# Layer 3's local attention: cosine products straight from PSUM in two halves, inverse norms by one power on GpSimd, and new instruction orders for slots 34 to 56

## The reference, cut to what matters

```python
qkv = h @ wqkv                      # 128 -> 3 x 512, eight heads of 64
q = l2norm(q) * qs; k = l2norm(k) * ksc
q = q * cos * scale + rotate_half(q) * sin * scale
k = k * cos / scale + rotate_half(k) * sin / scale
o = local_attention(q, k, v)        # windows of 64, each sees itself and the one before
def l2norm(t): return t / clip(norm(t), 1e-12)
```

## Time and profile before

| what | value |
|---|---|
| median of 3 runs | 3129.53 us (3119.51 to 3137.19) |
| span of the profiled execution | 3123.3 us |
| PE busy | 2749.7 us, 88% |
| DVE busy | 2224.2 us, 71% |
| ACT busy | 1703.5 us, 55% |
| POOL busy | 794.2 us, 25% |

### The profile page before, as it was taken

How to read it: one execution, slowest core, us unless ns; L and a number is a source line. 1 busy time by engine, 2 the same in 40 slices (tenths; PEclk the granted TensorE clock), 3 DMA queues, 4 the chain that set the end, 5 groups by cost and what they waited for, 6 DMA issues and landing times.

```text
span 3123.3 us, 66472 instructions
## 1 busy us (share of the span) xinstructions
PE 2749.7 (88%) x25741; PEld 1757.8 (56%) x25741; DVE 2224.2 (71%) x5316; ACT 1703.5 (55%) x4158; POOL 794.2 (25%) x809
## 2 busy tenths in 40 slices
PE   6878898899998899998878998999998889899998
PEld 3556665544455544467745887565653332455665
DVE  4766567788877677765566446889787777788884
ACT  2344533656622466543466434767765566767773
POOL 1010001111112111111232114646431112555550
PEclk8889997999999999998999989999999888999999
DMA  3523310000000000037500565010100000101001
GB/s 108 226 46 69 71 42 1 1 1 1 1 1 1 1 1 1 14 133 275 206 6 4 189 236 172 15 28 15 26 17 3 1 1 1 25 16 26 17 18 26
DMA packets 134803, 159.51 MB, mean 51 GB/s; under 512 B 82901, under 2 KB 109781, under 8 KB 132954
## 3 DMA queue, kind: packets, MB, share of 16 engines
q1 hardware_dynamic: 131962, 150.08, 15.7%
q0 software_dynamic: 2048, 4.20, 0.4%
q10 hardware_dynamic: 480, 0.98, 0.1%
HBM read 106.53 MB, written 30.61 MB: 44 GB/s over the span
## 4 chain that ended last, share of the span: by engine, by line
PE 47%; DVE 24%; ACT 10%; issue 8%; POOL 4%; DMA 3%; SPq 0%; DVEq 0%; POOLq 0%; ACTq 0%; another core or an unknown queue 0%
DVE nm L1221 5%; PE ps L1180 3%; PE ps L1955 3%; PE ps L1121 3%; PE ps L1157 3%; PE ps L565 3%; ACT hand L529 3%; PE ps L2157 3%; PE ps L418 2%; PE ps L2323 2%; PE ps L642 2%; DVE pre L2243 2%; PE ps L297 2%; PE ps L263 2%; PE ps L1551 1%
## 5 line engine op out<-in xcount | busy, mean ns | idle before, releaser
L1221 DVE TENSOR_REDUCE nm<-ps 128x2 f32<-128x256 f32 (+2 forms) x704 | 424.5, 637 | 87.1 <-PE ps L1121 50.1
L1270 ACT ACTIVATE core<-ps 128x512 f32<-128x512 f32 x672 | 359.1, 590 | 93.9 <-PE ps L1162 59.1
L359 POOL TENSOR_TENSOR rstd<-ve,weights 128x4 f32<-128x4 f32 x80 | 83.2, 1040 | 941.7 <-DVE ve L336 878.5
L2229 POOL TENSOR_TENSOR pre<-pre,sin 128x512 f32<-128x512 f32 x128 | 234.8, 1854 | 226.3 <-ACT pre L2200 199.6
L1121 PE MATMUL ps<-hand 128*128 128x128 bf16 (+4 forms) x1024 | 246.2, 315 | 44.0 <-DVE nm L1221 39.2
L529 ACT COPY hand<-ps 64x512 bf16<-64x512 bf16 x336 | 195.2, 581 | 126.7 <-PE ps L565 77.6
L1157 PE MATMUL ps<-hand 128*128 128x128 bf16 (+4 forms) x1024 | 223.0, 305 | 14.6 <-ACT hand L529 9.2
L2363 ACT ACTIVATE core<-ps,nm 128x128 f32<-128x128 f32 x512 | 182.5, 381 | 62.8 <-DVE nm L2380 62.0
L2234 POOL TENSOR_TENSOR ss<-ss,weights 128x16 f32<-128x16 f32 x64 | 195.9, 3061 | 71.0 <-DVE ss L2249 69.2
L2157 PE MATMUL ps<-weights,pre 128*128 128x512 f32 x384 | 203.2, 632 | 7.6 <-ACT pre L2203 4.5
L263 PE MATMUL ps<-identb 128*128 128x256 bf16 x1180 | 182.3, 283 | 18.3 <-PEq L3008 14.0
(11 more groups left out here) (348 smaller groups left out, 6693.3 us busy)
## 6 DMA issues: line engine op xcount, KB each, us to landing
hand<-in_experts SPq DMA_DIRECT2D x72, 836.0 KB, 6.7
shear<-post SPq DMA_DIRECT2D x64, 256.0 KB
core<-in_experts SPq DMA_DIRECT2D x16, 836.0 KB, 8.0
core<-shear SPq DMA_DIRECT2D x128, 64.0 KB, 2.2
hand<-hand SPq DMA_DIRECT2D x16, 512.0 KB, 4.4
hand<-hand SPq DMA_DIRECT2D x16, 384.0 KB, 5.6
pre<-sorted_in SPq DMA_DIRECT2D x8, 704.0 KB, 5.1
sorted_out<-core SPq DMA_DIRECT2D x88, 64.0 KB
```

Of the source, the lines that this page charges most:

```text
L1221: nc.vector.tensor_reduce(nm_of(unit), src, AX.X, ALU.max, negate=True).then_inc(negmax, 1)
L1270: nc.scalar.activation(prob8[:, i % PROBS, 0:w], m.ps[:, RING[at % NR], 0:w], ACT.Exp).then_inc(ring_out, 1)
L2229: ins = nc.gpsimd.tensor_tensor(o[:, :, :, z:z + hl], x[:, :, :, y0:y0 + hl], sn[:, t, :, z:z + hl].unsqueeze(2).to_broadcast([P, 2, LH, h ...
```

## The change

In `l3_layer_pre`:

- DVE's cosine product reads q and k from their PSUM banks instead of from `raw3`, in two instructions of 512 elements. Each waits until ACT has copied and squared the bank. PE may fill a bank that held q or k again only after this product (`rotated`).
- The inverse norm comes from POOL alone: a clamp of the sums of squares at 1e-24, then the power -0.5. The clamp and the reciprocal on DVE go.
- POOL's sine product of tile t waits for the addition of tile t-1 instead of its reciprocal; ACT's copy of tile t no longer waits for the cosine product of tile t-2.
- The constant 0.5 goes, and the constant -0.5 becomes wider.

The orders of slots 34 to 56 are new, those of the other slots the same (their text is only broken at other places). Core and finish are unchanged, and so is the preparation of the full attention.

```diff
+        def rotated(at):
+            for t in range(NT):
+                for i in range(2):
+                    if fill_of(t, i) == at:
+                        pe.wait_ge(cosed, 2 * t + i + 1)
...
             pe.wait_ge(lane.taken, max(at - N + 1, f))
+            rotated(at - N)
             nc.tensor.matmul(banks[at % N], s.hT[:, t * P:(t + 1) * P], qkv[:, l, i, :], start=True, stop=True).then_inc(lane.filled, 1)
...
             pe.wait_ge(lane.taken, at - N + 1)
+            rotated(at - N)
...
                         if i == 0 and t >= 2:
-                            act.wait_ge(cosed, t - 1)
                             act.wait_ge(sined, t - 1)
...
                     if t >= 1:
-                        pool.wait_ge(step, 3 * t)
+                        pool.wait_ge(step, t)
...
             pool.wait_ge(summed, t + 1)
-            nc.gpsimd.tensor_tensor(m.ss[:, 1, 0:2 * LH], m.ss[:, 0, 0:2 * LH], m.weight["half"][:, 0:2 * LH],
+            if t >= 1:
+                pool.wait_ge(roped, t)
+            nc.gpsimd.tensor_scalar(m.ss[:, 0, 64:64 + 2 * LH], m.ss[:, 0, 0:2 * LH], 1e-24, None, ALU.max).then_inc(held, 1)
+            pool.wait_ge(held, t + 1)
+            nc.gpsimd.tensor_tensor(m.ss[:, 1, 0:2 * LH], m.ss[:, 0, 64:64 + 2 * LH], m.weight["neg_half"][:, 0:2 * LH],
                                     ALU.pow).then_inc(rooted, 1)
...
-            yield T * t + 4.5
-            dve.wait_ge(copied, 2 * t + 2)
-            if t >= 2:
-                dve.wait_ge(lane.filled, fill_of(t - 2, 4) + 1)
-            nc.vector.tensor_tensor(heads(s.qt[:, t % 2, :]), heads(s.raw3[:, t % 2, :]),
-                                    cs[:, t, :, :].unsqueeze(2).to_broadcast(full), ALU.mult).then_inc(cosed, 1)
+            for i in range(2):
+                yield T * t + 3.0 + 1.7 * i
+                if t >= 2 and i == 0:
+                    dve.wait_ge(lane.filled, fill_of(t - 2, 4) + 1)
+                dve.wait_ge(lane.taken, fill_of(t, i) + 1)
+                nc.vector.tensor_tensor(heads(s.qt[:, t % 2, :])[:, i],
+                                        banks[fill_of(t, i) % N].rearrange("p (h e) -> p h e", e=LHD),
+                                        cs[:, t, i, :].unsqueeze(1).to_broadcast([P, LH, LHD]), ALU.mult).then_inc(cosed, 1)
...
             dve.wait_ge(rooted, t + 1)
-            nc.vector.tensor_scalar(m.ss[:, 0, 64:64 + 2 * LH], m.ss[:, 1, 0:2 * LH], 1e-12, None, ALU.max).then_inc(step, 1)
-            dve.wait_ge(step, 3 * t + 2)
-            nc.vector.reciprocal(m.ss[:, 1, 64:64 + 2 * LH], m.ss[:, 0, 64:64 + 2 * LH]).then_inc(step, 1)
-            dve.wait_ge(step, 3 * t + 3)
+            dve.wait_ge(step, t + 1)
             q = s.qt[:, t % 2, :].rearrange("p (h e) -> p h e", e=LHD)
-            nc.vector.tensor_tensor(q, q, m.ss[:, 1, 64:64 + 2 * LH].unsqueeze(2).to_broadcast([P, 2 * LH, LHD]),
+            nc.vector.tensor_tensor(q, q, m.ss[:, 1, 0:2 * LH].unsqueeze(2).to_broadcast([P, 2 * LH, LHD]),
                                     ALU.mult).then_inc(roped, 1)
```

The DVE stream of the preparation has four steps more in each slot (four tiles, one more cosine product each). As an example of the orders, PE and DVE of slot 38:

```diff
-    {"tensor": "c2a1c2a1b1a1b2a1b2a1b1a1b1a1b2c1b1c1a1c1b2c1b1a1c1b2c1b2c1a1b2a1c1b2",
-     "vector": "b3a1b1c1a1c1b1a1c2a1c1b2c1a1b1a1b1c1a1b2a1b4a1b1c1b1c1b1a1b2c1a1b2c1",
+    {"tensor": "c1a1c3b1a1b1a1b2a3b2c1a1c1b2a1c1b4c1a1b2c1b2c1a2b3c2b2",
+     "vector": "b3a1b2c1a1c1b1c2a1c1b1c1a1b1a2c1b4a1b1a1b5c1b1a2b4c2a1b2c1",
```

More of the change, by code:

```diff
@@ L57 @@
     [("ident", P), ("tri", P), ("causalT", P), ("blockdiag", P), ("tri8", NE * NE), ("rope_cos", NT * 4),
-     ("rope_sin", NT * 4), ("neg_half", NT), ("half", NT * 32), ("ones", P),
+     ("rope_sin", NT * 4), ("neg_half", NT * 8), ("ones", P),
      ("fills", NT), ("tiles", TILES)],
@@ L2131, in l3_layer_pre @@
     hl = LHD // 2
-    full = [P, 2, LH, LHD]
     f = lane.fills(5 * NT)
-    copied, shifted, summed, rooted, step, cosed, sined, roped = (lane.note(n) for n in (
-        "copied", "shifted", "summed", "rooted", "step", "cosed", "sined", "roped"))
+    copied, shifted, summed, rooted, step, cosed, sined, roped, held = (lane.note(n) for n in (
+        "copied", "shifted", "summed", "rooted", "step", "cosed", "sined", "roped", "held"))
     T = 9.0
@@ L2696 @@
      "sync": "a7b1a5"},
[L2697 to L2700, removed]
+    {"tensor": "e10b2e18a2b1a15b1a1b1a2e2a1e2b1a1e29",
+     "vector": "b11a2b3c1a1b1a9",
+     "scalar": "b2a9b2a2b1",
+     "gpsimd": "b1c1d1b1",
      "sync": "a6b1a6"},
[L2702 to L2710, removed]
+    {"tensor": "b3a1b1a2b1a2b1a1b1a1b1a1b1a1b1a2b1a1b1a1b1a1b1a1b1a1b1a5b1a1b4",
+     "vector": "b8a1b1a1b3a2b2a1b2a1b2a1b3a1c1a1b2a1b1a2b1",
+     "scalar": "b4a2b2a2b3a1b1a1b1a1b4a2b1a2b5",
+     "gpsimd": "b1c1b12d1",
+     "sync": "a12b1"},
+    {"tensor": "a2b1a1b2a1b1a1b2a2b5a1b6a2b2a1b2",
+     "vector": "b2a1b2a1b1a1b1a1b2a1b1a1b5a1b4a1c1b5a2b2a1",
+     "scalar": "a1b1a1b1a1b1a1b1a1b2a1b5a1b5a2b3a1b2",
+     "gpsimd": "c1b13d1",
@@ L2721 @@
      "sync": "c1b1"},
[L2722 to L2724 removed]
+    {"tensor": "c1b1a1c1a1b2c2a1b1a1b2a3b5c1a1c1b1c1b1a1b3c1a1c1b1a1b1c2b1c1b2",
+     "vector": "b1a2b1c1b1a1b1c1a1c2b1c1a2b2c1b3c1a1b2a1b2a1b2a1b3c1a1c2b2c1",
+     "scalar": "b1a1b2a2b1a1b2a2b5a1c2a1b2c1b3a1c1a1c1b5",
+     "gpsimd": "b5c1d1b7",
+     "sync": "c1b1"},
@@ new lines @@
+    {"tensor": "c1b1a1b2a1c3a1b3a2b3a1b1a1c1b1c1a1b1c1a1b2c1b2a1c1b1c1b2c1a1c1b2",
+     "vector": "b1a1b3a1c1a1b1c1b1c1a1c1b2a1c1b1c1a1c1b1a1b2a1b2a1b4c1b1c2b1a2b1c1",
+     "scalar": "b3a2b1a1b2a1b1a1b2a1b1c1a1b1c1a1b1c1a1b2c1b2c1a1b5",
+     "gpsimd": "b5c1b6d1b1",
+     "sync": "c1b1"},
+    {"tensor": "c1b1a1c2a1b1c1b1a1b3a2b1c1a2b2c1b2c1a1b2a1b3c2a1b2c1b1c2b2a1",
+     "vector": "b1a2c1b1c1b2a1c2b1c1a1c1b2c1a2b2a1b4a1b1a1b5c3a1b2c2a1",
+     "scalar": "b1a1b2a1b2a2b2a2c1b2c1b2a1c1a1b5c1a1c1b2a1b3",
@@ new lines @@
+    {"tensor": "a2c2a8c1a2c1b1a8b1a6b1a10b1a7c1a1b1a4c1a3c1a1c1a3c1a1b1a2b1a2c1b1a3b1a3b1a2c1b1a3b1a5c1a3b1a9",
+     "vector": "a1b1a2b1a4b1a3b1a10c2a14c1a1c2a2c1a3c1a7b1a2b6a1b1a1b1a1b1a1b1a2c1a2b1a2c1a3b1a2b1c1b1c2",
+     "scalar": "b2a8b1a12b1a2c1a3b1a2c1a2c1a1c2b1a1b2a2b1a5b1a6b1a8b1a14",
+     "gpsimd": "d1b2a2c1a1b4a1",
+     "sync": "c1"},
+    {"tensor": "a2b1a3c1a1b1a3c1a2b1a1c1a8b1a3c1a2b1a3c1a25b1a3b1a2b1a3b1a4b1a2b1a6b1a2c1a4b1a9",
+     "vector": "b4a5c1a4c1a11c1a2c1a4b1a2b2a3b1a2b1a2b1a1b1a3b1a4b1a5b1a2b1a5b1a6b1a3b1c1b1",
+     "scalar": "b3a1b1a3b1a7c1a7b1a2b2a12b1a4b1a7b1a7b1a16",
+     "gpsimd": "b3a2d1b3a2"},
@@ new lines @@
+    {"tensor": "a2b1a2c1a6b1a2c1a2b1a4c1a2b1a3b1a5c1a5c1a7c1a16b1a4b1a5b1a3b1a1b1a3b1a4b1a4b1a8",
+     "vector": "b4a10c1a3c1a7c1a7b1a2c1a3b1a1b1a2b1a2b1a2b1a2b1a4b1a3b1a3b1a1b1a9b1a3c1b3",
+     "scalar": "b4a5b1a5c1a12b1a1b2a12b1a8b1a4b1a8b1a11",
+     "gpsimd": "b1a3b5a1d1"},
+    {"tensor": "a2b1c1a2b1a4c1b1a2c1a1b1a2b1a10c1a9b1a3b1a1b1a4c1b1a4b1a3b1a5b2a1b1a4b1a3b1a3b1a4b1a4b1a3b1a3c1a4b1a"
+               "7",
+     "vector": "b4a2b1a2c1a2b1a1c1a3b1a1b1a8c1a2b1a1b1a7b1a2c1a1b1a1b1a4b1a4b1a3b1a5b1a2b2a4b1a2b1a3b1a4b3c1",
+     "scalar": "b5a9b1a4b1a3b1a2b1a3b1a3b1a3c1a2b1a1b1a3b1a1b1a3b1a5b1a2b1a5b1a3b1a6b1a8",
+     "gpsimd": "b3a1b2a1b3a1b4d1a1b1",
+     "sync": "b1"},
@@ L2805 @@
+    {"tensor": "a2b4a5b1a1b1a1b6a2",
+     "vector": "a2b2a2b4a2b1a2b3a1b2a2",
+     "scalar": "a7b1a1b4a2",
      "gpsimd": "c1b1",
      "sync": "b2"},
-    {"tensor": "a4b64a1b3a2b7a1b4a1b8a1b6a1b7a1",
+    {"tensor": "b7a4b69a1b6a1b3a1b1a2b5a1b2a1b3a1b3",
      "vector": "a12",
@@ L3271, in shape_constants @@
          "tri8": np.broadcast_to(np.tril(np.ones((NE, NE), f), -1).reshape(1, -1), (P, NE * NE)),
-         "neg_half": np.full((P, NT), -0.5, f), "half": np.full((P, NT * 32), 0.5, f), "ones": np.ones((P, P), f),
+         "neg_half": np.full((P, NT * 8), -0.5, f), "ones": np.ones((P, P), f),
          "fills": np.broadcast_to(P * np.arange(NT, dtype=f), (P, NT)),
```

215 lines of the change are left out of this document (89 added, 126 removed), and 8 rows, old and new, of the table SLOT_ORDERS.

## The result

The kernel after the change takes 3166.27 us (median of 4 runs, 3162.92 to 3181.76), the kernel before 3128.36 us beside it (3119.51 to 3137.19). The ratio is 1.0136, 95% interval 1.0102 to 1.0169: slower by more than the 0.5% that can be told from no change. The prediction said 3107 us, range 3077 to 3140, with 0.11 for slower. It was wrong in sign.

A forecast was written before the change was run, and what follows sets the result against it. In the fourteen slots PE and DVE were both near their limit, the cosine product 59% on the path. DVE's 30 us gain, less 4.5 for POOL's clamp and 2.5 for PE's waits, gave 23: 3107 us, range 3077 to 3140.

The forecast's parts named there:

- Orders. They change no amount of work.: Step on the new step orders: no gain or loss taken for the full attentions (2306 to 2588 us).
- 1% either way, 3 us: Margin allowed for the new orders in the full attentions, a stretch of 282 us.
- Two banks and a tile's period of 13 us leave room for it: in the sum nothing.: Step on PE refilling q and k banks only after DVE's half: up to 1.2 us later, priced at nothing.
- the bank is held too long: Rival: PE's refills wait for DVE's place in its queue; about 3152 us, case 3132 to 3160, chance 0.13.
- decision point of 0.30 us: Exposed PE wait for each cosine half at which the held bank makes the kernel measurably slower; 0.18 eats the gain.
- against it: The held-bank rival's counterargument: the order can put PE's fill of the bank later.
- 4.5 for POOL's clamp: Cost of the added clamp on POOL: 0.35 us a tile, 56 tiles, 0.23 of it on the path.
- 51 us x 59%: DVE's queue saving in the fourteen slots, 56 x (0.48 + 0.43), times the cosine product's path share: 30 us.
- no gain and no loss: Term for POOL's sine product losing its DVE neighbour: priced at zero, bound a gain of 1.2 us a tile.
- the 0.43 us of 56 tiles at 59%: DVE's cosine product as two PSUM halves: 1.65 to 1.22 us a tile, with 59% on the path.
- PE comes next: Rival: PE sets the pace once DVE is shorter, 3122 us; chance 0.26, shared with the dearer power.
- the three signs of being wrong: PE waiting over 20 us for halves; a 4 us power; fourteen slots still 725 us with PE over half the chain.

The follow-up runs named there:

- 29 moves: Changed code under the orders of before, with 29 DVE preparation steps moved ahead in twelve slots so DVE and PE don't block each other: 3268.6 us, ratio 1.0462.
- 1.0204: The change with its new orders and PE still waiting for the cosine halves, but the halves read raw3 in SBUF: 3190.6 us.
- 1.0210: The change with its new orders, but the halves read raw3 in SBUF and PE does not wait for them: 3197.7 us.
- the exchange of two steps: Kernel before with its orders; in each tile DVE forms the sums of squares before the cosine product: 3113.6 us, ratio 0.9964.

## Why the prediction was wrong

Four corners hold the answer:

| | orders of before | new orders |
|---|---|---|
| code before | 3125 | 3194 |
| code after | 3269 (with 29 moves) | 3166 |

**The step that failed: "Orders. They change no amount of work."** The sentence is true, and the busy rows confirm it. The conclusion "I take nothing" does not follow. Under the old code the new orders cost 69 us by the medians (62 by the ratio), and alone in the seven slots without changed code they cost 23, where "1% either way, 3 us" was meant to cover them. An order written out by hand fits one set of durations and waits; with another an engine can find at its head a step that isn't ready while others behind it are. That this is the way in which the time is lost is argued; shown are the time itself, the refills of the banks that come 1.8 us later, and a lower clock in the last slots.

**The code and its orders are one package.** The other failure is the sentence on the bank: "Two banks and a tile's period of 13 us leave room for it: in the sum nothing." Under orders close to the old ones reading PSUM with the hold costs 75 us net, and PE stands 143 us behind the halves. The rival "the bank is held too long" thus named the right resource, with 0.13; under those orders its decision point of 0.30 us exposed for each of the 128 halves was passed (143 / 128 = 1.1 us). That its 3152 us is near the 3166 measured is luck. In the change as it was made, PE's wait is 15.3 / 128 = 0.12 us a half and the hold is free (1.0204 against 1.0210): the new orders put the refills later, 3.5 us behind ACT's square instead of 1.7, as the rival's own "against it" says. What is paid is the orders. That they had to be as dear as they are is not shown: other orders for the same code may be cheaper, and in seven slots they certainly could be (15.5 us).

**The power part was priced at 56 x 0.48 x 0.59 = 16 us, less 4.5 for POOL's clamp, and gave nothing.** Removing 0.48 us a tile from DVE gave nothing under the old orders (1.0020) and nothing under the new ones (3166.0 against 3166.3). "51 us x 59%" took the chain's share of one instruction (the cosine product) for that of others. But the share wasn't far off: in the trace of before, clamp and reciprocal hold 12.5 us of the chain in the fourteen slots. With the power alone changed these are gone, and POOL's clamp and power hold 51.6 us of it where the power held 38.8: the path from the sums to the product exchanged 12.5 us on DVE for 12.8 on POOL. PE's part of the chain rose from 41% to 51%. So a share of the chain says what lies on it now, and not what the end gains when it goes. That the free time on DVE helped nobody else is argued, not shown.

**The cosine halves did gain, under the new orders.** From 1.0199 (old code) to 1.0127 (halves, old norms) it is 0.7% or 23 us by the ratios, 28 us by the medians; the prediction had the 0.43 us of 56 tiles at 59%, 14 us. The extra may come from the sine product, which got 0.4 us shorter a half in the mean and to which I gave "no gain and no loss"; no run parts it. The mechanism, two products in each other's way, is the one that holds: the same halves in SBUF cost 24 us more.

The Trainium skill (SBUF — State Buffer, Who interferes with whom) puts that collision on Vector instructions with two SBUF inputs. The runs agree: with one input in PSUM a half takes 0.683 us with hardly a spread, with both in SBUF 1.217 us in the mean.

**PE comes next** is neither right nor excluded. For it: the power alone gained nothing at 93% PE busy, and PE holds 63% of the chain in the fourteen slots after, one of the three signs of being wrong that the prediction had named, and the only one that came. Against it: the exchange of two steps took the fourteen slots to 709.5 us, with PE busy 671.5, and in the change PE is idle longer than before.

The sum with what was measured, from the medians: new orders +69, cosine halves from PSUM -28, power 0, hold 0 beside the new orders, together +41. The change measured beside before gives 38. These differences are between runs of different jobs, so each is good to some 10 us, and that they add up so well is in part luck.

Open: which of the moved steps in the sixteen slots carries the cost of the orders, and by what the orders lower the clock in the last ones. Halves from PSUM under the old orders without a hold weren't tried: there is no third bank for them.

## What to carry to other kernels

Price an order list like code: the test that tells most is the old code under the new orders, and it costs one run. When an edit holds a resource longer, ask what the engine in front of it must now do later, since the price may be paid in the order and not in any wait that the trace shows. Before splitting or moving an instruction to avoid a collision, try to exchange it with a neighbour that doesn't collide: two steps exchanged gave 14 us, where the rewrite lost 38.

## What the runs showed of the hardware

- Cutting a product of two SBUF inputs in half beside GpSimd's product doesn't halve it: 1.733 us for 1024 elements, 1.217 us for each 512 in the mean (0.656 at best, from PSUM 0.652).
- The collision reaches GpSimd's power too, with 16 elements for each partition: 2.90 us in the median before, 3.81 in the run in which the cosine product was placed behind the sums; 3.77 in the mean for the 44 that lie beside a cosine product, 3.15 for the 20 others.
- The exponent of the power makes no difference: 3.061 us in the mean for 0.5, 3.027 for -0.5.
- The same PE work ran at a granted clock of 1.00 or 0.91 in the last stretch, depending on the order of the steps alone; PE was busy 61.1 us or 66.4 with it.
